# A decoder stack on one core: second attention with keys absorbed per head and batch, and rotary halves added by GpSimd

## The reference

```python
kv_c = kv @ W_kvc                    # 64 keys per batch, 64 features
q_c = q @ W_dq                       # 256 queries per batch, 96 features
q_nope = (q_c @ W_uq).reshape(b, lq, H, HD).transpose(0, 2, 1, 3)     # 16 heads of 128
q_rope = (q_c @ W_qr).reshape(b, lq, H, R).transpose(0, 2, 1, 3)      # 16 heads of 64
k_nope = (kv_c @ W_uk).reshape(b, lk, H, HD)
k_rope = kv_c @ W_kr
q_rope, k_rope = _rope(q_rope, lq), _rope(k_rope, lk)
scores = (q_nope . k_nope + q_rope . k_rope) * scale
scores = where(key within seg_id - 8 .. seg_id, scores, -1e30)
attn = softmax(scores)
out = (attn @ (kv_c @ W_uv)) @ W_o
```

## Time and profile before

| | us |
|---|---|
| median of 3 runs | 1025.43 (1019.39 to 1025.76) |
| profiled execution, its time | 1024.47 |
| its span, first to last instruction | 1022.3 |
| PE busy | 878.7 (86%) |
| DVE busy | 702.5 (69%) |
| ACT busy | 486.4 (48%) |
| POOL busy | 416.9 (41%) |
| mean granted TensorE clock | 0.949 of 2.4 GHz |

### The profile page before, as it was taken

One profiled execution on the slowest core, in us unless ns is written; L12 is line 12 of the kernel. 1 busy time (PEld: TensorE's weight loads), 2 busy tenths in 40 slices (PEclk: granted clock), 3 DMA queues, 4 the chain that ended last, 5 costly groups with the idle time before them and its releaser, 6 DMA issues.

```text
span 1022.3 us, 14902 instructions
## 1 busy us (share of the span) xinstructions
PE 878.7 (86%) x5192; PEld 748.6 (73%) x5192; DVE 702.5 (69%) x1674; ACT 486.4 (48%) x1062; POOL 416.9 (41%) x776
## 2 busy tenths in 40 slices
PE   3576988986999779998767897999999899998997
PEld 2465877875888657886646786888888797797786
DVE  7678777777677766787886586655544876776534
ACT  5668746785467855676442353233322212212322
POOL 5758746577565576654252164211100080000000
PEclk9789999999999989999997797999999999999998
DMA  6000110010100110002010510321100120000001
GB/s 199 11 1 10 34 53 1 32 32 21 42 1 32 42 52 2 1 1 65 1 52 17 135 52 5 133 75 47 32 1 1 37 63 1 1 1 1 1 1 42
DMA packets 26170, 33.93 MB, mean 33 GB/s; under 512 B 4848, under 2 KB 18992, under 8 KB 25968
## 3 DMA queue, kind: packets, MB, share of 16 engines
q1 hardware_dynamic: 24816, 30.00, 9.8%
q10 hardware_dynamic: 1280, 2.98, 0.8%
HBM read 31.93 MB, written 1.05 MB: 32 GB/s over the span
## 4 chain that ended last, share of the span: by engine, by line
PE 48%; DVE 28%; ACT 11%; POOL 7%; issue 5%; DMA 0%; ACTq 0%; DVEq 0%
PE PS L712 14%; PE PS L786 7%; POOL raw L2012 3%; PE PS L879 3%; PE PS L576 3%; DVE cat L1393 3%; DVE st L1489 3%; ACT P L1021 2%; PE PS L834 2%; PE PS L604 2%; PE PS L667 2%; ACT raw L993 2%; DVE yb L1389 2%; PE PS L850 2%; PE PS L625 2%
## 5 line engine op out<-in xcount | busy, mean ns | idle before, releaser
L2012 POOL TENSOR_SCALAR raw<-raw,mvq,rsq 128x128 f32<-128x128 f32 x320 | 176.6, 566 | 1.7
L712 PE MATMUL PS<-xq,WH 128*128 128x512 f32 x480 | 153.2, 401 | 0.0
L576 PE MATMUL PS<-WH,xq 128*128 128x256 f32 (+1 forms) x256 | 97.2, 395 | 44.9 <-DVE xq L1393 19.3
L1021 ACT ACTIVATE P<-PS,sm 128x256 f32<-128x256 f32 x128 | 60.1, 482 | 88.9 <-DVE sm L1553 88.9
L712 PEld LDWEIGHTS PS<-xq,WH 128*128 128x128 f32 x480 | 88.7, 193 | 16.1
L576 PEld LDWEIGHTS PS<-WH,xq 128*128 128x128 f32 x256 | 55.1, 215 | 58.7 <-issue 30.0
L712 PE MATMUL PS<-xq,WL 128*128 128x512 f32 x240 | 94.7, 395 | 0.0
L576 PE MATMUL PS<-WL,xq 128*128 128x256 f32 (+1 forms) x256 | 90.3, 368 | 0.0
L667 PE MATMUL PS<-PH,cat 128*128 128x256 f32 x256 | 69.0, 304 | 20.5 <-DVE cat L1393 20.0
L786 PE MATMUL PS<-xq,m_hh 128*128 128x256 f32 x384 | 78.4, 304 | 6.2 <-DVE m_hl L1806 4.5
L1553 DVE TENSOR_REDUCE sm<-PS 128x2 f32<-128x512 f32 x64 | 43.9, 686 | 56.6 <-PE PS L604 56.2
(11 more groups left out here) (280 smaller groups left out, 2293.7 us busy)
## 6 DMA issues: line engine op xcount, KB each, us to landing
wst<-in_wgu SPq DMA_DIRECT2D x24, 256.0 KB, 2.8
wst<-in_wall SPq DMA_DIRECT2D x18, 256.0 KB, 3.1
dst<-in_wdn SPq DMA_DIRECT2D x24, 128.0 KB, 2.0
wst<-in_wkvx SPq DMA_DIRECT2D x8, 256.0 KB, 3.0
m_pre<-in_wo ACTq DMA_DIRECT2D x1, 2048.0 KB, 8.4
wst<-in_fgu SPq DMA_DIRECT2D x6, 256.0 KB, 2.8
P<-in_wall SPq DMA_DIRECT2D x5, 256.0 KB, 7.4
l_KZ<-in_wproj SPq DMA_DIRECT2D x4, 256.0 KB, 3.9
```

The source lines that it names most:

```text
L576: t = e.matmul(PS[:, b, o:o + n], xq[s][:, k, c * 128:(c + 1) * 128], W[:, k, w0:w0 + n], start=(k == 0 and i == 0), stop=(k == 1 and i == 1))
L712: t = e.matmul(PS[:, b, :], W[wi][:, gu, k, :], a[:, k, cols], start=(n == 0), stop=(n == 5))
L1021: t = e.activation(P_[:, c, :], PS[:, b, c * 256:(c + 1) * 256], ACT.Exp, bias=m[:, 0, c:c + 1], accum_out=m[:, 1, c:c + 1])
L2012: t = e.tensor_scalar(v, v, mvq[:, par, n, 0:1], rsq[:, par, n:n + 1], ALU.add, ALU.mult)
```

## The change

The scores' compressed part is no longer taken from a query that was multiplied by the absorbed weight; the keys are multiplied by it instead. `absorb` now makes W_uk W_uq^T per head (64x96, `AT`, four banks and four copies in place of two). A new step `keymix` after `outmix` makes for each head 96x256 from `AT` and the compressed keys of all batches: 16 products of 256 columns in eight banks, copied by ScalarE to `KM`. `queries` makes only the rotary part: per pair of heads one product with `wqr` and one with `wrt` in the two halves of one bank, so 16 products and eight banks a batch where there were 24 and twelve, and no part 2. `turn_q` multiplies a whole bank by cosines and sines in one instruction into one of three buffers `tq`, and a new GpSimd step `add_q` adds the two halves (128x256) into `QR`; VectorE waits before it writes a buffer until the sum three before it is done. `scores2` waits for the sums of its batch, and makes per bank one product of the compressed query with 512 columns of `KM` and four of `QR` with 128 columns.

GpSimd does the nine FFN weight tiles (`load_f`, the old loop body) between groups of four sums. `wqr` and `wrt` are loaded later, by ScalarE's queue during the experts, into the buffer that the early experts have left; `QR`, two of the `tq` buffers and the router's `OH`, `OT`, `RR` share memory with tiles that are dead or not yet live. The copy of rotary keys to the lower half of `KA` falls away.

```diff
@@ moe_order
     do("outmix")
+    do("keymix")
@@ late_order
-            for part in range(3):
+            for part in range(2):
                 do("queries", 0, part)
...
-        if more:
-            do("queries", bb + 1, 2)
@@ tensor
             def absorb():
-                w.wait_ge(q_in, 64)
-                for z in range(2):
+                w.wait_ge(q_in, 32)
+                for z in range(4):
                     b = fill(("aw", z))
-                    for h in range(8 * z, 8 * z + 8):
-                        t = e.matmul(PS[0:96, b, h % 8 * 64:h % 8 * 64 + 64], wuq[:, h, :], wuk[:, h, :], start=True, stop=True)
+                    for h in range(4 * z, 4 * z + 4):
+                        t = e.matmul(PS[0:64, b, h % 4 * 96:h % 4 * 96 + 96], wuk[:, h, :], wuq[:, h, :], start=True, stop=True)
...
+            def keymix():
+                for z in range(8):
+                    b = fill(("km", z))
+                    emptied(("aw", z // 2))
+                    for h in (2 * z, 2 * z + 1):
+                        t = e.matmul(PS[0:96, b, h % 2 * 256:h % 2 * 256 + 256], AT[:, h, :], KA[0:64, :], start=True, stop=True)
+                    t.then_inc(full[b], 1)
...
-                for p in (range(4 * part, 4 * part + 4) if part < 2 else range(4)):
-                    b = fill((("qa" if part < 2 else "qb"), bb, p))
-                    for hh in range(2):
-                        W = aw[:, 2 * p + hh, :] if part < 2 else wrt[:, (2 * p + hh) * 128:(2 * p + hh + 1) * 128]
-                        t = e.matmul(PS[:, b, hh * 256:(hh + 1) * 256], W, qcT[:, bb * 256:(bb + 1) * 256], start=True, stop=True)
+                w.wait_ge(r_in, 32)
+                for p in range(4 * part, 4 * part + 4):
+                    b = fill(("qr", bb, p))
+                    for z, W in enumerate((wqr, wrt)):
+                        t = e.matmul(PS[:, b, z * 256:(z + 1) * 256], W[:, p * 128:(p + 1) * 128],
+                                     qcT[:, bb * 256:(bb + 1) * 256], start=True, stop=True)
                     t.then_inc(full[b], 1)
...
+                w.wait_ge(added.sem, added.at[bb, 7])
                 for z in range(2):
                     b = fill(("ls", c, z))
+                    e.matmul(PS[:, b, :], qcT[:, c * 128:(c + 1) * 128],
+                             KM[0:96, bb, 8 * z:8 * z + 8, :].rearrange("p h t -> p (h t)"), start=True, stop=False,
+                             skip_group_check=True)
                     for p in range(4 * z, 4 * z + 4):
-                        e.matmul(PS[:, b, p % 4 * 128:p % 4 * 128 + 128], QB[bb % 2][:, p, cc:cc + 128],
-                                 KZ[:, bb, :, :].rearrange("p a t -> p (a t)"), start=True, stop=False, skip_group_check=True)
-                        for o in range(2):
-                            t = e.matmul(PS[:, b, p % 4 * 128 + o * 64:p % 4 * 128 + o * 64 + 64],
-                                         QA[bb % 2][:, 2 * p + o, cc:cc + 128], KA[:, bb * 64:(bb + 1) * 64],
-                                         start=False, stop=True, skip_group_check=True)
+                        t = e.matmul(PS[:, b, p % 4 * 128:p % 4 * 128 + 128], QR[bb % 2][:, p, cc:cc + 128],
+                                     KZ[:, bb, :, :].rearrange("p a t -> p (a t)"), start=False, stop=True,
+                                     skip_group_check=True)
@@ scalar
+                if (j, h) == (NPRE + 1, 0):
+                    w.emptied(("c", j, h))
+                    e.dma_start(wqr, A["wqr"]).then_inc(r_in, 16)
+                    e.dma_start(wrt, A["wrt"]).then_inc(r_in, 16)
...
+            for z in range(8):
+                b = w.filled(("km", z))
+                copy(KM[0:96, :, 2 * z:2 * z + 2, :].rearrange("p b h t -> p h b t"),
+                     PS[0:96, b, :].rearrange("p (h b t) -> p h b t", h=2, b=4)).then_inc(free[b], 1)
@@ vector
+                for p in range(4 * part, 4 * part + 4):
+                    n = 8 * bb + p
+                    b = w.filled(("qr", bb, p))
+                    if n > 2:
+                        w.wait_ge(added.sem, added.at[(n - 3) // 8, (n - 3) % 8])
+                    e.tensor_tensor(tq[n % 3], PS[:, b, :], tb_[:, 0:512], ALU.mult).then_inc(free[b], 1)
...
-                if more:
-                    turn_q(bb + 1, 2)
-                if bb:
                     split_f(bb - 1)
@@ gpsimd
+            def add_q(bb, part):
+                if bb > 1:
+                    w.filled(("ls", 2 * bb - 3, 1))
+                for p in range(4 * part, 4 * part + 4):
+                    n = 8 * bb + p
+                    w.emptied(("qr", bb, p))
+                    e.tensor_tensor(QR[bb % 2][:, p, :], tq[n % 3][:, 0:256], tq[n % 3][:, 256:512],
+                                    ALU.add).then_inc(added.sem, 1)
+
+            w.wait_ge(downed.sem, downed.at[MOE[-1]])
+            w.filled(("bp", 3))
+            for bb in range(4):
+                for part in range(2):
+                    add_q(bb, part)
+                    if bb:
+                        load_f(2 * bb + part - 2)
+            for j in range(6, 9):
+                load_f(j)
```

More of the change, by code:

```diff
@@ L372, in program @@
                 qcT = sb("l_qcT", [96, 1024], F32, cl)
-                QA = [sb(f"l_QA{i}", [128, 16, 256], F32, cl) for i in range(2)]
-                QB = [sb(f"l_QB{i}", [128, 8, 256], F32, cl) for i in range(2)]
+                tq = [prea[:, 8, :], prea[:, 9, :], sb("l_tq", [128, 512], F32, cl)[:]]
                 S = [sb(f"l_S{i}", [128, 1024], F32, cl) for i in range(2)]
@@ L408, in program @@
             "weigh": lambda j, h: ([("g", j, h), ("u", j, h)] if j >= NPRE else []) + [("c", j, h)],
[L409 removed]
+            "outmix": lambda: [("bp", z) for z in range(4)], "keymix": lambda: [("km", z) for z in range(8)]}), (0, 1, 2, 3))
         B.ring(fills(moe_order, {
[L411 removed]
+            "xs": lambda bb: [("xs", bb)], "logits": lambda: ["lg"], "absorb": lambda: [("aw", z) for z in range(4)],
             "turn_oh": lambda: [("oh", 0), ("oh", 1)], "rows": lambda: [("rr", 0), ("rr", 1)],
@@ L417, in program @@
             "turn": lambda bb: [("lt", bb)], "compress": lambda bb: [("qc", bb)],
-            "queries": lambda bb, part: [("qa", bb, p) for p in range(8)][4 * part:4 * part + 4] if part < 2
-            else [("qb", bb, p) for p in range(4)],
+            "queries": lambda bb, part: [("qr", bb, p) for p in range(4 * part, 4 * part + 4)],
             "scores": lambda c: [("ls", c, 0), ("ls", c, 1)], "turn_p": lambda c: [("lp", c, 0), ("lp", c, 1)],
@@ L469, in program @@
         masked = sem("masked")
+        added = count("added", [(bb, p) for bb in range(4) for p in range(8)])
         subbed_l = count("subbed_l", range(8))
@@ L1213, in scalar @@
                 if n == 3:
-                    for z in range(2):
+                    for z in range(4):
                         b = w.filled(("aw", z))
-                        w.wait_ge(q_in, 64)
-                        copy(aw[:, 8 * z:8 * z + 8, 0:64], PS[0:96, b, :].rearrange("p (h c) -> p h c", h=8)).then_inc(free[b], 1)
+                        copy(AT[:, 4 * z:4 * z + 4, :], PS[0:64, b, 0:384].rearrange("p (h c) -> p h c", h=4)).then_inc(free[b], 1)
                 if n == 1:
@@ L2085, in gpsimd, with load_f @@
                 load_dn(j + 8)
-            w.wait_ge(downed.sem, downed.at[MOE[-1]])
-            for j in range(9):
+            def load_f(j):
                 src, landed, value = staged(("f", j))
```

51 lines of the change are left out of this document (19 added, 32 removed).

## The result

The changed kernel takes 1028.95 us, the median of 20 runs (1025.75 to 1030.88); the kernel before, run beside it on the same chip, 1024.06 us (20 runs, 1019.39 to 1026.91). The ratio is 1.0045, with a 95% interval of 1.0033 to 1.0057: slower by about 4.6 us. The prediction was 1024.5, no change, with a range of 1016 to 1031. The time lies in the range, but it is not "no change": the measurement tells 0.45% from none, where the prediction took 1% as its limit.

The account below looks back on a forecast made before the run. TensorE, busy 86% of the span, was taken as the bound, with VectorE close behind. Chain -7.8 us, clock +6.7 and GpSimd beside VectorE +0.3 gave -0.8 on the profiled 1024.47; predicted 1024.5, range 1016 to 1031.

Parts of the forecast that it names:

- TensorE's durations: TensorE's work in the second attention: scores 3.42 us a half batch (-1.88), queries -3.51 a batch, keymix +7.02 once.
- the chain: Walk through the second attention without clock loss: batch 0 +1.63 us, batches 1 and 2 31.40 each, batch 3 -1.88.
- rival that scores don't get as short: In scores, products of 128 columns take 0.33 us: +5.8 us, 1030; chance 0.08.
- Before the first scores: From outmix to the first scores: keymix +7.02, queries -3.51, so +3.51 us; GpSimd's sums at 0.75 cost nothing.
- slower, by GpSimd: GpSimd sums over 0.88 us delay first scores and batch 0's groups; subtractions and divisions wait: +8.1 us, 1033; chance 0.12.
- Batches 0 and 1: Batch 0 +1.63 us with a TensorE wait of 6.3; batch 1 -3.76 with 4.97 waiting for the layer norm.
- Clock: TensorE at half rate after waits in batches 0 to 2, 2.1 us each, and 0.4 more for the fourth: +6.7.
- it hardly falls: TensorE's clock hardly falls after the waits: -7.5 to -5 us, 1017 to 1020; chance 0.15.
- stays down much longer: TensorE's clock costs 3.4 us per wait, 11.9 for 6.7: +5.2 us, 1030; chance 0.10.
- GpSimd beside VectorE: Sums and FFN tiles under VectorE's softmax: +0.3 us in batch 0; slack of 0.85 covers it in batches 1 and 2.
- the sum: Total over the kernel: -7.8 + 6.7 + 0.3 = -0.8 us on the profiled 1024.47.
- three signs of being wrong: In the second attention: clock stays at 1.00 across the waits, VectorE waits for sums, or a batch under 30 us.

## Why the prediction was wrong

- **TensorE's durations: right.** Keymix 7.07 (7.02), a half batch of scores 3.5 (3.42), batches 1 and 3 within 0.4 of the chain. The rival that scores don't get as short falls.
- **Before the first scores: right.** +3.6 for +3.51. GpSimd's sums took 0.73 each (0.75), and VectorE never waited for one. The rival "slower, by GpSimd" named the right engine and the wrong place: it put the decision at a sum over 0.88 us and the price into late sums and the softmax.
- **Batches 0 and 1: right.** Waits of 6.10 and 4.83 (6.3, 4.97); the work taken from TensorE became waiting.
- **Clock: right.** 2.33 measured in batch 1 against 2.1 taken. In the changed kernel the steps behind the three waits took 2.45, 2.26 and 1.90 us longer than at full speed (7.88 for 5.43, 6.16 for 3.90, 5.80 for 3.90), and turn_p and project in batch 3 took 9.52 us before and after: 6.6 in all, for 6.7. The rivals that it hardly falls, or stays down much longer, fall.
- **GpSimd beside VectorE: the step that failed.** The prediction had +0.3 here, for the subtractions and divisions of batch 0. It wrote that "three are left after the last sums, a batch before the FFN" and asked only whether these tiles would be late for the FFN, not what runs beside them. They ran under batch 2's layer norm: +4.55 from project's end to f_turn (10.42 for 5.87), where it had nothing; in batch 0, where it had its 0.3, VectorE's chain kept its length (838.50 to 856.05, 17.55 us for 17.6). The rule was cited, and applied to instructions of 1024 elements alone. A chain of 15 tiny steps is hit harder: each step can wait for a whole GpSimd instruction, 0.46 to 1.12 us for 0.16. With 4.6 in place of 0.3 the sum would have been +3.5; with the tiles held back, outmix to the end is the same as before, 213.5 for 213.4, where the sum had -1.1 without the 0.3. None of the prediction's three signs of being wrong came true, because none of them looked at VectorE's small steps. And that 1028.95 still lies in the range is luck: the range reached up to 1031 for a slower clock and longer scores, and neither came.
- **Left over.** The medians differ by 4.9 us, the traces by 3.7 from outmix on. `absorb`, which the prediction put at nothing, is a small part of the rest: from the eight products of the earlier trace rows to the router's transposes it is 30.75 to 30.77 us in the nine traces of the new attention and 30.52 or 30.53 in the three of the old, so about 0.24. The other 1.8 of the 2.06 us by which outmix starts later is mostly scatter between executions: 1.6 of it is there at the long wait near 255 us (256.77 for 255.16), and the run with the last tiles held back, which differs from the changed kernel by one wait much later, has 255.30 there. About 0.9 us between the medians stays unexplained.

## What to carry to other kernels

When an engine off the critical path is given new work, its old work moves too: follow every instruction to the end of its queue and ask what runs beside it, above all a chain of tiny dependent VectorE steps (a layer norm), where each step can wait for a whole GpSimd instruction. Work taken from a bound engine may have been the cover of a wait: look for what of the kernel's own can fill the hole, since here a bare wait of 5 us was paid twice, as a wait and in the clock behind it, and moving one elsewhere made it dearer.

## What the runs showed of the hardware

- VectorE steps of 128x2 are held by GpSimd just as large ones are. Under memsets of 0.53 us tensor_scalar steps took up to 0.55 and tensor_tensor steps 0.16; under multiplications of 0.62 us they took up to 0.51 and 0.47; under tiles, whose subtraction lasts 1.26, they took up to 1.11 and 1.12.
- What TensorE's clock does is not told by the length of the last wait alone. In the kernel before it fell after a wait of 1.90 us; with f_turn late in that kernel, a wait of 1.89 in the same place brought no fall:

```profile
938.25 1.09 PE L858 MATMUL PS<-idf,l_S 128*128 128x128 f32 x8 [1.89 <-DVE l_S L1887]
939.18 7.07 PE L877 MATMUL PS<-l_Bp,l_x2T 128*128 128x256 f32 x32
```

  It fell after 1.63 us ahead of the first scores, and in batch 0, with the useless products in its wait, after two gaps of 0.96 and 0.94. Values behind a fall took from 4.68 us (with the memsets) to 6.58 (with project first). The prediction's 2.1 a fall was a good mean over places, and no more than that.
